# Sorting edges inside a language-model tower: larger pieces in the sort's trips through memory, ten dealing places, joint minimum and maximum operations

## The chip, the cores and the metric

The kernel runs on one core of a Trainium2 chip. A core has TensorE (PE, matrix products), VectorE (DVE, elementwise work and reductions), ScalarE (ACT, functions), GpSimd (POOL, here mostly indirect transfers) and SyncE (SP, which here only issues DMAs), and 16 DMA engines. The metric is the device time of one execution in microseconds (us). The kernel before has a median of 4921.01 us over 3 runs, from 4919.95 to 4923.06. The profile is of one further execution, which took 4925.54 us; its span from the first to the last instruction is 4923.8 us.

## The reference, cut to what matters

Two layers over 16,384 tokens of 64 features, all in float32. Each line adds to `h`:

```python
h = _L0_tok_ref(x, ...)                        # embedding and a small network
h = h + _L0_attn_ref(_layernorm(h), ...)       # a recurrence over 64 rows of 256 tokens
h = h + _L0_ffn_ref(_layernorm(h), ...)        # 8 experts, the best 2 per token
h = h + _L1_attn_ref(_layernorm(h), ...)       # attention in windows of 64
h = h + _L1_ffn_ref(_layernorm(h), ..., edge_index)
```

The last one is a graph layer, and it is what the sort is for. Each of 262,144 edges goes from a source token to a target token, and every target takes a softmax over its edges:

```python
e = leaky_relu(a_src[src] + a_dst[dst], negative_slope=0.2)
e_max = segment_max(e, dst, num_segments=M)
ee = exp(e - e_max[dst])
denom = segment_sum(ee, dst, num_segments=M)
agg = segment_sum(h[src] * (ee / (denom[dst] + 1e-16))[:, :, None], dst, num_segments=M)
```

The kernel sorts the edges by target, so that the segment sums become scans along sorted edges.

## The kernel before, in words

**Stages.** The tokens are worked on in two halves. For each half: 8 iterations of the recurrence (each two lanes of 512 tokens), a norm, 8 blocks of the experts, a norm, 16 iterations of attention, a norm, and a table of one row per token (`node_table`), which SP stores. When the first half's table is stored, GpSimd starts the edge work: 960 indirect gathers of table rows for the edges whose source lies in the first half, while the other engines do the second half; then it scatters target terms, gathers the rows of the other edges (1088), and gathers the segment ends (256). VectorE scans the rows as they come.

**The sort** runs beside the first half on VectorE. The keys (target, source and a flag in one word) lie as 128 partitions x 2048 in one of two buffers `K`, and it is a bitonic merge sort by a list of 192 steps from `network()`:

- `x`: an exchange at distance `d` along the 2048 keys of a partition, from one buffer to the other. For the first ten levels (55 steps, `up` not zero) the direction alternates along the row, and the step is four operations of 512 elements per partition (lines 1073, 1074); for the others it is one minimum and one maximum of 1024 elements (lines 1068, 1069).
- `sign`: one multiplication (line 1089) that turns the direction of a partition.
- `move`: keys of different partitions have to meet, so the buffer makes a trip through memory. VectorE only raises a signal (the copy at line 1092); SP waits for it, stores the buffer as it stands (`sort2`, line 314), waits until that has landed (line 315), and loads it back as 16-element pieces (`sortx`, line 316). There are 14 moves, two for each of 7 levels of merging across partitions. The next exchange waits for the load.

At the end come 3 more instructions (lines 1096 to 1098) that pick pivots; then `pivots()` counts them with TensorE, and its result (`key_block_idx`) starts GpSimd's 256 search gathers (line 457), which VectorE uses in attention (`search_round`).

**What sets the order.** Each engine has its own program, and the engines wait for one another by semaphores. VectorE's program is written out by hand: in `it(i)` each `step(...)` is one instruction for each of two lanes, preceded by its waits, and `burst(k)` puts sort steps in between. How many go where is worked out ahead by `sort_plan()` into `REC_AT` (recurrence: 7 places in each of 8 iterations), `PRE_AT` (before the experts), `FFN_AT` (4 quarters in each of 8 blocks of the experts) and `LEFT` (behind the experts). The plan assumes a time per step and per move, and deals no step before the move ahead of it should be over. SP works through its DMAs in program order, the gates of the experts among them, so that a move's wait stands in front of what follows in the queue.

The plan of before, as steps (moves) per iteration of the recurrence: 25, 25, 20 (2), 14 (1), 16 (2), 16 (2), 7 (1), 17 (2); 3 before the experts; 46 (4) in the experts; 4 behind them.

## Time and profile before

| | us |
|---|---|
| median of 3 runs | 4921.01 |
| the profiled execution, device time | 4925.54 |
| its span, first to last instruction | 4923.8 |
| 8 iterations of the recurrence, first half (36 to 790) | 754 |
| experts, first half (866 to 1093.5) | 227.5 |
| rest of the sort, pivots, norm (1093.5 to 1192) | 98.5 |
| attention, norm and table, first half (1192 to 1566) | 374 |
| from there to the end | 3357.8 |
| VectorE busy in the whole span | 2325.4 (47%) |
| GpSimd busy in the whole span | 2769.7 (56%) |

The stretches are cut by the starts of instructions in the trace, and the profiled execution's own time is the one that they belong to. A busy share over the whole span says little here: GpSimd does nothing in the first 1157 us and is the busiest engine behind them. The chain of work that ended last goes back from the last instruction, at each step to what released it. "issue" is time in which an engine waited for nothing that the profile shows.

### The profile page before, as it was taken

To read this page: it belongs to the slowest core of one execution; us is meant where nothing else is said; L and a number is where in the kernel's file an instruction comes from. 1 tells how busy PE (TensorE), PEld (TensorE's weight loads), DVE (VectorE), ACT (ScalarE), POOL (GpSimd) and SP (SyncE) were. 2 spreads that over 40 slices of the span, in tenths; PEclk is the share of its full clock that TensorE was granted. 3 is DMA by queue.
4 is the path that set the end of the run, shared out by engine and by line. 5 is a ranking of instruction groups with operands and counts; after the bars stand their busy time and mean duration, and the time that the engine had idled before them with its cause. 6 is when DMAs were issued, how large, how long until landed. Compare 5 with 4: busy or idle time off the path is not lost.

```text
span 4923.8 us, 70771 instructions
## 1 busy us (share of the span) xinstructions
PE 2410.7 (49%) x27920; PEld 1760.6 (36%) x27920; DVE 2325.4 (47%) x5102; ACT 1150.2 (23%) x2612; POOL 2769.7 (56%) x2870
## 2 busy tenths in 40 slices
PE   4666766764885788869688200024242424332000
PEld 3555655223663666753376100013131312121000
DVE  8867665778774344454677100023333242422336
ACT  2232332322442344435454000001010111100000
POOL 0000000004772777777777777777777777776775
PEclk8888887876886899979899555555555555555555
DMA  2033342750002911116211200112121212211122
GB/s 79 6 44 40 52 49 35 127 84 24 26 25 30 29 33 27 29 21 135 43 16 23 59 2 2 39 40 70 45 65 46 63 46 63 53 44 46 43 61 75
DMA packets 351882, 226.11 MB, mean 46 GB/s; under 512 B 215599, under 2 KB 311696, under 8 KB 349136
## 3 DMA queue, kind: packets, MB, share of 16 engines
q1 hardware_dynamic: 254272, 164.52, 16.9%
q0 software_dynamic: 92464, 49.28, 6.8%
q10 hardware_dynamic: 4896, 8.92, 0.7%
q8 instruction: 166, 2.72, 0.2%
q14 instruction: 84, 0.69, 0.1%
HBM read 136.08 MB, written 86.40 MB: 45 GB/s over the span
## 4 chain that ended last, share of the span: by engine, by line
POOL 50%; issue 19%; DVE 17%; PE 10%; DMA 3%; ACT 1%; POOLq 0%; SPq 0%; DVEq 0%
POOL arena L487 21%; POOL arena L470 19%; PE bank L501 10%; POOL arena L497 5%; POOL edge_dst_terms L479 5%; DVE arena L1069 3%; DVE arena L1068 2%; DMA arena<-sort_exchange 1%; DVE arena L1074 1%; DVE arena L1073 1%; DVE arena L1350 1%; DVE arena L1355 1%; DMA sort_exchange<-arena 0%; DVE arena L1203 0%; DVE arena L1079 0%
## 5 line engine op out<-in xcount | busy, mean ns | idle before, releaser
L501 PE MATMUL bank<-arena 64*64 64x64 f32 (+12 forms) x25222 | 2111.6, 291 | 1782.5 <-ACT arena L967 1184.0
L501 PEld LDWEIGHTS bank<-arena 64*64 64x64 f32 (+4 forms) x25222 | 1492.5, 164 | 2383.3 <-ACT arena L967 1257.3
L487 POOL DMA_INDIRECT arena<-node_table,arena x1088 | 1033.7, 950 | 331.6 <-issue 331.6
L470 POOL DMA_INDIRECT arena<-node_table,arena x960 | 942.1, 981 | 292.9 <-issue 292.3
L457 POOL DMA_INDIRECT arena<-sorted_keys,key_block_idx x256 | 257.1, 1004 | 444.4 <-DVE key_block_idx L1208 366.7
L450 POOL IOTA arena<- 128x1024 int32 x1 | 1.0, 989 | 781.6 <-DVE h_res L1153 781.6
L969 ACT ACTIVATE bank<-bank 128x512 f32<-128x512 f32 x32 | 18.6, 582 | 1413.5 <-DVE bank L1411 1413.5
L501 PE MATMUL bank<-ident,arena 128*128 128x128 f32 (+2 forms) x1792 | 235.2, 301 | 157.3 <-ACT arena L952 77.4
L1403 DVE COPY arena<-arena 128x4 f32<-128x4 f32 x32 | 5.8, 182 | 647.5 <-DMA arena<-node_table,arena 647.0
L497 POOL DMA_INDIRECT arena<-sums_sorted,arena x256 | 263.5, 1029 | 79.1 <-issue 77.7
L479 POOL DMA_INDIRECT edge_dst_terms<-arena x256 | 251.9, 984 | 84.5 <-issue 84.5
L501 PEld LDWEIGHTS bank<-ident,arena 128*128 128x128 f32 (+2 forms) x1792 | 209.8, 183 | 189.8 <-DVE arena L1356 104.2
L937 ACT ACTIVATE arena<-bank,arena 128x512 f32<-128x512 f32 x256 | 161.9, 684 | 220.4 <-PE bank L501 220.4
L1418 DVE TENSOR_TENSOR_SCAN arena<-bank,arena 128x64 f32<-128x64 f32 x640 | 179.0, 373 | 1.1
L1387 DVE TENSOR_TENSOR arena<-bank,arena 128x512 f32<-128x512 f32 x64 | 44.3, 692 | 267.2 <-PE bank L501 267.2
L1396 DVE COPY arena<-arena 128x4 f32<-128x4 f32 x1 | 0.2, 170 | 347.7 <-DMA arena<-edge_dst_terms 347.7
L1068 DVE TENSOR_TENSOR arena<-arena 128x1024 f32<-128x1024 f32 x116 | 141.7, 1221 | 37.6 <-DMA arena<-sort_exchange 34.9
L1312 DVE SCALAR_TENSOR_TENSOR arena<-bank,arena 128x512 f32<-128x512 f32 x128 | 90.2, 746 | 140.1 <-PE bank L501 81.2
L1069 DVE TENSOR_TENSOR arena<-arena 128x1024 f32<-128x1024 f32 x116 | 141.2, 1217 | 0.0
L967 ACT ACTIVATE arena<-bank,arena 128x512 f32<-128x512 f32 x128 | 84.5, 687 | 215.5 <-PE bank L501 215.3
L952 ACT ACTIVATE arena<-arena 128x512 f32<-128x512 f32 x128 | 77.5, 630 | 197.7 <-DVE arena L1356 197.7
L1350 DVE TENSOR_TENSOR arena<-bank,arena 128x512 f32<-128x512 f32 x128 | 80.0, 683 | 45.6 <-ACT arena L950 45.1
(377 smaller groups left out, 2789.2 us busy)
## 6 DMA issues: line engine op xcount, KB each, us to landing
arena<-expert_gates SPq DMA_DIRECT2D x64, 512.0 KB, 7.6
arena<-node_table,arena POOLq DMA_INDIRECT x2048
sums_sorted<-arena SPq DMA_DIRECT2D x32, 768.0 KB, 3.3
expert_out<-arena SPq DMA_DIRECT2D x64, 256.0 KB, 2.5
arena<-expert_out SPq DMA_DIRECT2D x16, 1024.0 KB, 5.6
sort_exchange<-arena SPq DMA_DIRECT2D x14, 1024.0 KB, 3.9
early_rows<-arena POOLq DMA_DIRECT2D x15, 768.0 KB
arena<-early_rows SPq DMA_DIRECT2D x15, 768.0 KB
```

The costliest lines, as they stand in the source:

```text
L457: G.indirect_dma_start(out=rows[:,u,:],out_offset=None,in_=keysb,in_offset=bass.IndirectOffsetOnAxis(ap=idx2[:,t:t+1],axis=0)).then_inc(s_ ...
L470: G.indirect_dma_start(out=early_b[j%2][:,c,:],out_offset=None,in_=tbl, in_offset=bass.IndirectOffsetOnAxis(ap=gidx[:,j*CW+c:j*CW+c+1],axi ...
L479: G.indirect_dma_start(out=ad_e,out_offset=bass.IndirectOffsetOnAxis(ap=sidx[:,h*NT+t:h*NT+t+1],axis=0), in_=nodeG[:,t,20:24],in_offset=No ...
L487: G.indirect_dma_start(out=rch[:,j%NB,c,:],out_offset=None,in_=tbl, in_offset=bass.IndirectOffsetOnAxis(ap=gidx[:,CA+j*CW+c:CA+j*CW+c+1],a ...
L497: G.indirect_dma_start(out=at[:,t,:],out_offset=None,in_=sums_d,in_offset=bass.IndirectOffsetOnAxis(ap=eidx[:,h*NT+t:h*NT+t+1],axis=0)).th ...
L501: mm=lambda o,a,b,st=True,sp_=True: nc.tensor.matmul(o,a,b,start=st,stop=sp_,skip_group_check=True)
L937: A.activation(B.hT[:,n%2,:],B.ps[n%2][:,:],ACT.Gelu,bias=fb1[:,n%8:n%8+1]).then_inc(B.ge,1)
L1068: V.tensor_tensor(y[:,:,0,:],x[:,:,0,:],x[:,:,1,:],ALU.min)
L1069: lk(V.tensor_tensor(y[:,:,1,:],x[:,:,0,:],x[:,:,1,:],ALU.max))
L1312: V.scalar_tensor_tensor(out=B.tm[:,q%2,:] if q else B.acc[:,k%2,:],in0=B.ps[2+m%2][:,:],scalar=fb2[l][:,q:q+1],in1=B.G[:,k%2,q,:],op0=ALU ...
L1350: step(lambda B,l:V.tensor_tensor(B.K,B.ps[0][:,P+D:2*P].unsqueeze(1).broadcast_to((P,8,D)),h8(hmask),ALU.mult),"act:q")
L1418: last=V.tensor_tensor_scan(R[:,:,f],xe[:,0,:,head(f)],R[:,:,f],cin[:,f:f+1],ALU.mult,ALU.add)
```

## The change

It touches only the sort, in four places. (1) In a move of level j the pieces have 2048/2^j keys instead of 16. On the way out (odd moves) they are stored as pieces and loaded as whole rows; on the way back (even moves) they are stored as whole rows and loaded as pieces. The distances of the exchanges between the two moves change with it. (2) Of the 55 exchanges in alternating directions 27 are written as one minimum and one maximum over 1024 elements. (3) `burst` has ten places instead of seven: one ahead of each of the three U additions is new, and the fifth stands four steps later. `sort_plan()` deals with other assumptions. (4) Behind the experts, the first steps up to the last move come ahead of the norm, the other 12 and the pivots behind it.

The new plan, as steps (moves) per iteration of the recurrence: 29, 29, 12 (2), 13 (1), 13 (1), 11 (2), 13 (1), 12 (1); 2 (1) before the experts; 43 (4) in the experts; 4 (1), then 12, behind them. By place, the first two iterations have 9, 2, 6, 3, 4, 1, 1, 1, 1, 1, and the fifth has 3, 0, 3, 1, 2, 1, 1, 1, 0, 1.

```diff
-        steps+=[("sign",j,0),("move",2*j-1,0)]+[("x",16<<b,0) for b in range(j-1,-1,-1)]
+        steps+=[("sign",j,0),("move",2*j-1,0)]+[("x",(RC>>j)<<b,0) for b in range(j-1,-1,-1)]
...
-PLACES=((2.0,9),(29.0,2),(40.0,5),(53.0,3),(64.0,4),(80.0,1),(92.0,1))
+PLACES=((1.7,8.0,(9,9,5,4)),(17.0,3.5,(2,2,1)),(24.0,6.0,(6,6,3)),(37.0,2.0,(3,3,1)),(46.0,4.0,(4,4,2)),
+        (52.5,2.0,(1,)),(55.0,2.0,(1,)),(57.5,2.0,(1,)),(62.0,0.3,(1,1,0)),(66.0,1.5,(1,)))
+REC_LEN=68.0; MOVE=[12.0]*8+[14.0]*2+[16.0]*2+[19.0]*2+[0.0]; FFN_LEN=22.0
...
-        sort2=sort_d.rearrange("(p c) -> p c",p=P); sortx=sort_d.rearrange("(p q l) -> q p l",p=P,q=P)
+        sort2=sort_d.rearrange("(p c) -> p c",p=P); sortx=[sort_d.rearrange("(q p l) -> p q l",p=P,q=1<<j) for j in range(XL+1)]
...
-                        sp.dma_start(sort2,K[k]).then_inc(s_st,16)
+                        j=(n+1)//2; parts=lambda t: t.rearrange("p (q l) -> p q l",q=1<<j)
+                        if n%2: sp.dma_start(sortx[j],parts(K[k])).then_inc(s_st,16)
+                        else: sp.dma_start(sort2,K[k]).then_inc(s_st,16)
                         sp.wait_ge(s_st,16*n)
-                        sp.dma_start(K[1-k].rearrange("p (q l) -> p q l",l=16),sortx).then_inc(s_sl,16)
+                        if n%2: sp.dma_start(K[1-k],sort2).then_inc(s_sl,16)
+                        else: sp.dma_start(parts(K[1-k]),sortx[j]).then_inc(s_sl,16)
...
+                    def part(t,at,step): return bass.AP(tensor=t.tensor,offset=t.offset+at,ap=[list(t.ap[0])]+[[st,n] for st,n in ((2*up,RC//(2*up)),(step,2),(2*d,up//(2*d)),(1,d)) if n>1])
+                    if 2*up==RC or up==2*d or d==1:
+                        lo,hi=part(x,0,up),part(x,d,up)
+                        V.tensor_tensor(part(y,0,up+d),lo,hi,ALU.min)
+                        lk(V.tensor_tensor(part(y,d,up-d),lo,hi,ALU.max))
...
                 for c in range(1,4):
+                    burst(4+c)
                     step(lambda B,l:V.tensor_tensor(B.U[:,c,:],B.ps[2][:,c*D:(c+1)*D],B.Wy[:,c,0,:],ALU.add),f"pe:U{c}","dve:W")
...
                 if part==0:
-                    steps_of((LEFT,0))
+                    steps_of((LEFT[0],0))
+                norm(part,H,xn)
+                if part==0:
+                    steps_of((LEFT[1],0))
                     pivots()
-                norm(part,H,xn)
```

What this moves on VectorE, in the order of its program. First the fifth iteration of the recurrence (counted from one) around the U additions, which are line 1142 of the kernel before and line 1169 of the changed one; lines 1139, 1140 and 1165, 1166 are the two additions ahead of them. Before:

```order
L1135 TENSOR_TENSOR arena<-arena 128x256 x2
L1136 TENSOR_TENSOR arena<-arena 128x256 x2
L1137 TENSOR_TENSOR arena<-arena 128x256 x2
L1138 TENSOR_TENSOR arena<-arena 128x256 x2
L1139 TENSOR_TENSOR arena<-bank,arena 128x512 x2
L1140 TENSOR_TENSOR arena<-bank,arena 128x512 x2
L1142 TENSOR_TENSOR arena<-bank,arena 128x64 x6
```

Now, with exchanges at lines 1088 and 1089:

```order
L1165 TENSOR_TENSOR arena<-bank,arena 128x512 x2
L1166 TENSOR_TENSOR arena<-bank,arena 128x512 x2
L1088 TENSOR_TENSOR arena<-arena 128x64x16
L1089 TENSOR_TENSOR arena<-arena 128x64x16
L1169 TENSOR_TENSOR arena<-bank,arena 128x64 x2
L1088 TENSOR_TENSOR arena<-arena 128x128x8
L1089 TENSOR_TENSOR arena<-arena 128x128x8
L1169 TENSOR_TENSOR arena<-bank,arena 128x64 x2
L1088 TENSOR_TENSOR arena<-arena 128x256x4
L1089 TENSOR_TENSOR arena<-arena 128x256x4
L1169 TENSOR_TENSOR arena<-bank,arena 128x64 x2
```

Three exchanges moved in between additions that stood in a row.

Then VectorE behind the experts: line 1299 (now 1326) adds the last expert results, lines 1096 to 1098 are the sort's last step, line 1203 and those ahead of it belong to the pivots; lines 1201 to 1206 are the norm of the changed kernel. Before:

```order
L1299 TENSOR_TENSOR h_res<-h_res,bank 128x4x64 x2
L1068 TENSOR_TENSOR arena<-arena 128x256x4
L1069 TENSOR_TENSOR arena<-arena 128x256x4
L1068 TENSOR_TENSOR arena<-arena 128x512x2
L1069 TENSOR_TENSOR arena<-arena 128x512x2
L1068 TENSOR_TENSOR arena<-arena 128x1024
L1069 TENSOR_TENSOR arena<-arena 128x1024
L1096 TENSOR_SCALAR pivot_ints<-arena 128x32
```

Now, from the last of the three exchanges that follow the experts:

```order
L1088 TENSOR_TENSOR arena<-arena 128x64x16
L1089 TENSOR_TENSOR arena<-arena 128x64x16
L1118 COPY rowbase<-rowp_f 128x1
L1201 TENSOR_REDUCE ln_stat<-h_res 128x32
L1202 SCALAR_TENSOR_TENSOR arena<-ln_stat,h_res 128x2048
L1204 TENSOR_REDUCE ln_stat<-arena 128x32
L1206 TENSOR_TENSOR arena<-arena,ln_stat 128x2048
L1201 TENSOR_REDUCE ln_stat<-h_res 128x32
L1202 SCALAR_TENSOR_TENSOR arena<-ln_stat,h_res 128x2048
L1204 TENSOR_REDUCE ln_stat<-arena 128x32
L1206 TENSOR_TENSOR arena<-arena,ln_stat 128x2048
L1088 TENSOR_TENSOR arena<-arena 128x1024
```

The norm, which stood behind the pivots, now stands between the last move (line 1118) and the eleven exchanges that follow it.

## Rows read from the trace of the kernel before

**Rows 1.** The chain that ended last, by line (page, part 4): shares of the span.

```profile
POOL arena L487 21%; POOL arena L470 19%; PE bank L501 10%; POOL arena L497 5%; POOL edge_dst_terms L479 5%; DVE arena L1069 3%; DVE arena L1068 2%; DMA arena<-sort_exchange 1%; DVE arena L1074 1%; DVE arena L1073 1%; DVE arena L1350 1%; DVE arena L1355 1%; DMA sort_exchange<-arena 0%; DVE arena L1203 0%; DVE arena L1079 0%
```

**Rows 2.** Busy time by stretch: stretch, length, PE, PEld, DVE, ACT, POOL, granted clock, DMA, GB/s.

```profile
36.00:790.00 754.00, 500.48 (x8896) 432.08 (x8896) 541.39 (x986) 231.38 (x561) 0.77 (x1) 0.83 0.24 34
...
866.00:1093.50 227.50, 161.53 (x600) 54.66 (x600) 175.04 (x214) 73.46 (x116) 0.00 (x0) 0.82 0.68 105
...
1566.00:4923.80 3357.80, 1390.75 (x14346) 993.57 (x14346) 1200.36 (x3011) 652.69 (x1413) 2506.20 (x2583) 0.63 0.23 45
...
2236.00:2385.00 149.00, 140.62 (x597) 44.70 (x598) 79.41 (x127) 73.45 (x116) 114.98 (x114) 0.96 0.61 124
```

**Rows 3.** GpSimd in order of time: start, duration (us), engine, line, operation [idle before, releaser].

```profile
1566.98 0.18 POOL L462 TENSOR_TENSOR pool_spare<-pool_spare 1x1 f32<-1x1 f32 x1 [75.22 <-DMA node_table<-arena]
```

**Rows 4.** Busy time by stretch, first and last of five iterations in the second half.

```profile
1747.60:1815.50 67.90, 55.77 (x1112) 47.66 (x1112) 29.81 (x77) 28.65 (x70) 51.86 (x54) 0.95 0.15 31
...
2024.40:2092.30 67.90, 55.60 (x1112) 47.48 (x1112) 29.92 (x78) 28.60 (x70) 51.66 (x55) 0.95 0.15 31
```

**Rows 5.** Busy time by stretch, two iterations of the recurrence in the first half.

```profile
143.40:249.30 105.90, 63.90 (x1112) 55.82 (x1112) 90.44 (x178) 28.90 (x70) 0.00 (x0) 0.81 0.03 6
...
611.20:693.00 81.80, 60.00 (x1112) 51.99 (x1112) 43.47 (x90) 28.76 (x70) 0.00 (x0) 0.87 0.45 47
```

**Rows 6.** VectorE in order of time, one iteration of the second half (no sort).

```profile
1757.35 0.43 DVE L1114 TENSOR_SCALAR arena<-arena 128x512 f32<-128x512 f32 x1 [8.10 <-ACT arena L867]
...
1762.64 0.86 DVE L1117 TENSOR_SCALAR arena<-bank 128x256 f32<-128x256 f32 x2 [1.35 <-PE bank L501]
1765.90 0.88 DVE L1118 SCALAR_TENSOR_TENSOR arena<-bank,arena 128x256 f32<-128x256 f32 x2 [2.40 <-ACT arena L877]
1777.39 0.69 DVE L1127 TENSOR_TENSOR arena<-bank,arena 128x512 f32<-128x512 f32 x1 [5.94 <-PE bank L501]
...
1787.00 0.42 DVE L1133 TENSOR_TENSOR arena<-bank,arena 128x256 f32<-128x256 f32 x1 [1.91 <-PE bank L501]
...
1796.97 0.69 DVE L1139 TENSOR_TENSOR arena<-bank,arena 128x512 f32<-128x512 f32 x1 [3.85 <-PE bank L501]
...
1802.29 0.39 DVE L1142 TENSOR_TENSOR arena<-bank,arena 128x64 f32<-128x64 f32 x2 [1.87 <-PE bank L501]
```

**Rows 7.** VectorE in order of time, first operations of two exchanges in four operations.

```profile
44.20 0.69 DVE L1073 TENSOR_TENSOR arena<-arena 128x512 f32<-128x512 f32 x1
...
46.73 0.69 DVE L1073 TENSOR_TENSOR arena<-arena 128x512 f32<-128x512 f32 x1
```

**Rows 8.** VectorE in order of time: sort's rest (two-operation exchanges), norm, line 1211.

```profile
1093.83 1.23 DVE L1068 TENSOR_TENSOR arena<-arena 128x1024 f32<-128x1024 f32 x1 [0.30 <-DVE h_res L1299]
...
1096.23 1.23 DVE L1068 TENSOR_TENSOR arena<-arena 128x1024 f32<-128x1024 f32 x1
...
1156.55 2.28 DVE L1174 TENSOR_REDUCE ln_stat<-h_res 128x32 f32<-128x2048 f32 x1
...
1180.42 1.23 DVE L1211 TENSOR_SCALAR arena<-arena 128x2048 int32<-128x2048 int32 x1
```

**Rows 9.** SP and TensorE in order of time around the move at 642 us.

```profile
647.89 0.67 SPq L316 DMA_DIRECT2D arena<-sort_exchange  x1
...
663.45 11.06 PE L501 MATMUL bank<-arena 64*64 64x64 f32 x198 [5.63 <-issue]
```

**Rows 10.** DMA issues: out<-in, queue, operation, count, KB each, median us to landing.

```profile
sort_exchange<-arena SPq DMA_DIRECT2D x14, 1024.0 KB, 3.9
...
arena<-sort_exchange SPq DMA_DIRECT2D x14, 0.1 KB, 14.2
...
end_positions<-arena SPq DMA_DIRECT2D x1, 128.0 KB
```

**Rows 11.** Waits between 862 and 1105 us: us in total, times, longest.

```profile
DVE arena L1068 <- DMA arena<-sort_exchange: 27.9, 4, 7.1
```

**Rows 12.** Waits of the SP queue, whole span.

```profile
SPq L369 <- DMA end_positions<-arena: 60.4, 1, 60.4
```

More of the change, by code:

```diff
@@ L65, in network, with take @@
     for j in range(1,XL+1):
-        steps+=[("sign",j,0),("move",2*j-1,0)]+[("x",16<<b,0) for b in range(j-1,-1,-1)]
+        steps+=[("sign",j,0),("move",2*j-1,0)]+[("x",(RC>>j)<<b,0) for b in range(j-1,-1,-1)]
         steps+=[("move",2*j,0)]+[("x",1<<b,0) for b in range(LOC-1,-1,-1)]
     return steps
-PLACES=((2.0,9),(29.0,2),(40.0,5),(53.0,3),(64.0,4),(80.0,1),(92.0,1))
-BEFORE_FFN=2
+PLACES=((1.7,8.0,(9,9,5,4)),(17.0,3.5,(2,2,1)),(24.0,6.0,(6,6,3)),(37.0,2.0,(3,3,1)),(46.0,4.0,(4,4,2)),
+        (52.5,2.0,(1,)),(55.0,2.0,(1,)),(57.5,2.0,(1,)),(62.0,0.3,(1,1,0)),(66.0,1.5,(1,)))
+REC_LEN=68.0; MOVE=[12.0]*8+[14.0]*2+[16.0]*2+[19.0]*2+[0.0]; FFN_LEN=22.0
 def sort_plan():
-    net=[kind for kind,d,up in network()]+["move"]
-    at=0; ready=0.0
-    def take(now,most):
-        nonlocal at,ready
-        n=m=0
-        while n<most and at<len(net) and now>=ready:
-            now+=2.4; n+=1
-            if net[at]=="move": ready=now+20.0; m+=1
+    net=network()+[("move",2*XL+1,0)]
+    at=0; now=38.0; ready=0.0
+    def take(most,hidden):
+        nonlocal at,now,ready
+        n=m=0; t=now
+        while n<most and at<len(net) and t>=ready:
+            kind,d,up=net[at]
+            t+=2.6 if up else dict(x=2.45,sign=1.4,move=0.2)[kind]; n+=1
+            if kind=="move": ready=t+MOVE[d-1]; m+=1
             at+=1
+        now=max(now,t-hidden)
         return n,m
-    rec=[[take(i*100.0+t,most) for t,most in PLACES] for i in range(ITA)]
-    t=ITA*100.0+10.0
-    pre=[take(t+30.0*k,3) for k in range(BEFORE_FFN)]
-    t+=30.0*BEFORE_FFN
-    ffn=[[take(t+36.0*k+9.0*q,2) for q in range(4)] for k in range(ITA)]
-    left=len(net)-at
-    return rec,pre,ffn,left
+    rec=[]
+    for i in range(ITA):
+        row=[]; prev=0.0
+        for off,hidden,most in PLACES:
+            now+=off-prev; prev=off
+            row.append(take(most[min(i,len(most)-1)],hidden))
+        now+=REC_LEN-prev
+        rec.append(row)
+    pre=[]
+    for t,most in ((22.0,0),(30.0,3)):
+        now+=t; pre.append(take(most,5.0))
+    now+=20.0
+    ffn=[]
+    for k in range(ITA):
+        row=[]
+        for q in range(4):
+            now+=FFN_LEN/4; row.append(take(2,2.0))
+        ffn.append(row)
+    rest=[kind for kind,d,up in net[at:]]
+    first=rest.index("move")+1
+    return rec,pre,ffn,(first,len(rest)-first)
 REC_AT,PRE_AT,FFN_AT,LEFT=sort_plan()
@@ L1070, in exchange @@
                 else:
-                    x,y=(t.rearrange("p (g u b w d) -> p g u b w d",u=2,b=up//(2*d),w=2,d=d) for t in (x,y))
-                    for u in range(2):
-                        V.tensor_tensor(y[:,:,u,:,0,:],x[:,:,u,:,0,:],x[:,:,u,:,1,:],ALU.max if u else ALU.min)
-                        last=V.tensor_tensor(y[:,:,u,:,1,:],x[:,:,u,:,0,:],x[:,:,u,:,1,:],ALU.min if u else ALU.max)
-                    lk(last)
+                    def part(t,at,step): return bass.AP(tensor=t.tensor,offset=t.offset+at,ap=[list(t.ap[0])]+[[st,n] for st,n in ((2*up,RC//(2*up)),(step,2),(2*d,up//(2*d)),(1,d)) if n>1])
[3 more added lines that the diff above has]
+                        lk(V.tensor_tensor(part(y,d,up-d),lo,hi,ALU.max))
+                    else:
+                        x,y=(t.rearrange("p (g u b w d) -> p g u b w d",u=2,b=up//(2*d),w=2,d=d) for t in (x,y))
+                        for u in range(2):
+                            V.tensor_tensor(y[:,:,u,:,0,:],x[:,:,u,:,0,:],x[:,:,u,:,1,:],ALU.max if u else ALU.min)
+                            last=V.tensor_tensor(y[:,:,u,:,1,:],x[:,:,u,:,0,:],x[:,:,u,:,1,:],ALU.min if u else ALU.max)
+                        lk(last)
             def below(t0,n,w,keys,c,out):
@@ L1133, in it @@
                 step(lambda B,l:V.tensor_tensor(B.dta[:,:,:],c4(B.ps[0][:,T:2*T]),B.dtb[:,:,:],ALU.add),"pe:x4","dve:d2")
-                step(lambda B,l:V.tensor_tensor(B.dtb[:,:,:],c4(B.ps[1][:,T:2*T]),B.dta[:,:,:],ALU.add),"pe:x8","dve:d4"); burst(4)
+                step(lambda B,l:V.tensor_tensor(B.dtb[:,:,:],c4(B.ps[1][:,T:2*T]),B.dta[:,:,:],ALU.add),"pe:x8","dve:d4")
                 step(lambda B,l:V.tensor_tensor(B.gtb[:,:,:],B.V[:,:,:],s4(B.bon[:,:]),ALU.mult),"act:bons")
@@ L1137, in it @@
                 step(lambda B,l:V.tensor_tensor(B.gtb[:,:,:],B.gtb[:,:,:],B.gt[:,:,:],ALU.mult),"act:gts","dve:gb")
-                step(lambda B,l:V.tensor_tensor(B.gt[:,:,:],B.gt[:,:,:],r4(rows[:,3,:],0),ALU.mult),"dve:gtb")
+                step(lambda B,l:V.tensor_tensor(B.gt[:,:,:],B.gt[:,:,:],r4(rows[:,3,:],0),ALU.mult),"dve:gtb"); burst(4)
                 step(lambda B,l:V.tensor_tensor(B.Z1[:,:,:,:],v3(B.ps[1][:,:]),B.Z0[:,:,:,:],ALU.add),"pe:Z1")
```

4 lines of the change are left out of this document (2 added, 2 removed).

## The prediction

> **What bounds the kernel now.** I read the chain of work that ended last first: its largest pieces are GpSimd's row gathers, lines 487, 470, 497 and 479 [rows 1]. The table of stages shows where they lie: from 1566 us to the end GpSimd is busy for 2506 of 3358 us, one indirect transfer after another [rows 2]. Nothing in that stretch is touched. It starts when GpSimd's wait of 75.22 us for the node table of the first half ends, at 1567 us [rows 3]. So the end follows the moment at which the table is stored, and before it lies a chain on TensorE, VectorE and ScalarE: 8 recurrence iterations (36 to 790 us), the first half's experts (866 to 1093.5 us), the sort's rest, the pivots and a norm (to 1192 us), attention (to 1566 us). VectorE deals the sort's 192 steps into this chain. What a step costs is what it takes beyond a gap in which VectorE would have waited anyway.
>
> The size of the gaps is in the second half, which runs the same loops without a sort: its undisturbed iterations take 68 to 70 us, 68.9 on average over five [rows 4], and its eight expert blocks 149 us [rows 2]. With the sort, the iteration from 143.4 us takes 105.9 us and the one from 611.2 us 81.8 us [rows 5], the expert blocks 227.5 us [rows 2]. That is the room: 753 against 551 us, 227.5 against 149 us.
>
> **A model of one iteration.** In an iteration without sort VectorE waits 8.10 us before line 1114 and 1.35 more before 1117 (some 10.5 us with three waits of under 0.6 us between), 2.40 before 1118, 5.94 before 1127, 1.91 before 1133, 3.85 before 1139, and 1.87 before each of the three U additions at 1142 [rows 6]; before 1150 and 1153 there is little (I take 0.5 and 1.6). An exchange in four operations repeats every 2.53 us [rows 7], one in two operations every 2.40 us [rows 8]. A place costs its steps less its gap, and not less than zero. For the iteration from 143.4 us (9, 2, 5, 3, 4, 1, 1 steps of 2.53) that is 12.3+2.7+6.7+5.7+6.3+2.1+0.9 = 36.7, with 68.9 it makes 105.6 us against 105.9 measured. So the model holds where no move runs. In iterations 2 to 7 it leaves 33 us unexplained, and these are the ones with moves: TensorE stands 5.63 us with nothing that the profile shows to wait for [rows 9], while the load of a move keeps the DMA engines full.
>
> **Part 1, ten places and another deal.** The recurrence gets 132 steps instead of 140. Iterations 0 and 1 get 29 each instead of 25, the others 11 to 13 instead of 7 to 20, and the three new places lie in the U gaps. Iterations 0 and 1: 9, 2, 6, 3, 4 and five single steps of 2.46 (half of them joint) cost 39 us, so 108 us each, 2 us more than now; with the 2 us by which the first is longer today that is 217.6. Iterations 2 to 7: 5 steps at the first place cost 1.5, 4 or 3 nothing; one at the second nothing; three at the third 1.2; one at the fourth 0.5; two at the fifth 0.9; a step before each U 0.5; one at the last 0.8. That gives 71.7, 71.5, 73.9, 72.5, 71.5, 73.9 = 435 us. Sum 652.6 against 753.1 now: 100.5 us less if no move disturbs. Moves still run: 8 instead of 10, of about 9 instead of 18 us (part 2), so of the 33 us I keep 33 x 0.8 x 0.47 = 12. **Term 1: -88 us, from -100 (no disturbance left) to -67 (all of it left).** The joint operations are in this: 27 of 55 exchanges become 0.13 us shorter, 3.5 us in all; a form of theirs that the trace does not show could cost nothing more, since the two and the four operation form differ only by their number.
>
> **Part 2, the moves.** Now every move stores 8 KB rows in 3.9 us and loads 64-byte pieces in 14.2 us [rows 10]: the same megabyte, 16,384 pieces, so small pieces are dear. After it, level j moves in pieces of 8192/2^j bytes, on the store side going out and on the load side coming back. As an estimate, linear in the pieces between those two rows, a side takes 4 us at levels 1 to 3, 5.2 at level 4, 6.5 at 5, 9 at 6, 14.2 at 7; with the other side and 0.5 us of signals a move takes 9 to 10 us at levels 1 to 4, 11, 13.5 and 18.6 at 5, 6 and 7. The deal leaves at least 13 us between a move and the next step in the recurrence, so VectorE should not wait there. In the expert blocks it now waits 27.9 us on four moves [rows 11]. Placed on the natural rhythm, the 43 steps there cost 50 us and the 46 of now 51 (the model gives 148.7+50.7+27.9 = 227.3 against 227.5 measured), and the gaps left for the four moves are 12.5, 14, 14 and 16 to 18 us. Only the store of level 7 should be late, by about 3 us. SP waits for each store before it loads, and the gates' loads queue behind; those are issued a block of 18 us ahead, so a store of up to 14 us is covered.
>
> The trace has no small stores of this size. The nearest row is a store of 32,768 single words, behind which SP waits 60.4 us [rows 10, 12], 1.84 us per thousand: 16,384 pieces would take at most 30 us by it, 14.2 us if a store costs what a load does. I take the second, the nearer in piece size; at the other end the last two stores make VectorE wait some 20 us longer. The Trainium skill has a rule against this change, in "DMA: Bandwidth & Descriptors", section Specifications: under 512 bytes a DMA engine reads, modifies and writes. No run here shows it yet; if it doubled the store of level 7, the forecast below would rise by about 14 us, inside the range. **Term 2: -25 us, from -28 to -5.**
>
> **Part 3, what is left.** 16 steps instead of 4 lie behind the expert blocks. Three and the last move come first, then the norm (24 us [rows 8], from 1156.55 us on, until 1180.4), under which the last move's 18.6 us are hidden; if it took 30 us, 6 would show. Then 11 exchanges of 2.40 us stand open: 26.4 us. The pivots themselves and SP's store ahead of them are unchanged. **Term 3: +26.5 us, from +25 to +32.** Since the norm now stands ahead of the pivots, GpSimd's search starts 24 us nearer to the table; its spare time there is 75 us [rows 3], so 51 are left and nothing is late. The step before the experts gets two steps instead of three, which a wait for TensorE hides in both cases: nothing.
>
> **Sum.** -88 - 25 + 26.5 = -86.5 us, on the profiled execution's 4925.5 us: 4839. The median of the runs, 4921.0, lies 4.5 us below that execution, so 4834.5. The bounds together give 4818 to 4879. The shift reaches the end whole, because both GpSimd's gathers and the second half of the dense work start from the table.
>
> **Rivals.**
> (a) The moves stay as long as now, because the piece is not what the DMA pays for. Against it: the two rows of one megabyte. Then VectorE waits 25 us in the recurrence (18 us per move against gaps of 13 to 15), the other 21 us of disturbance stay, and the expert blocks wait 14 us longer: +60, 4894.
> (b) Slower: a step costs the average wherever it stands, because VectorE's late answer also holds up TensorE and its clock (the granted clock is 0.81 in the iteration from 143.4 us, 0.87 in the one from 611.2 us [rows 5]). Today the recurrence pays (753-551)/140 = 1.44 us a step and the experts (227.5-149)/46 = 1.71. Then 132 and 43 steps give -12 and -5, and with +26.5 the kernel is 10 us slower: 4931. It turns slower from 1.37 us a step in the recurrence on. Against it: the model's 105.6.
> (c) The short gaps cost less than I count, no move disturbs anything and the clock stays at the second half's 0.95 [rows 4]: 4810.
>
> **Chances.** Forecast 0.77, (a) 0.09, (b) 0.06, (c) 0.08. The range reaches to (a) and to the better end of the forecast: 4815 to 4895. A measurement of this kernel tells about 0.2% (10 us) from no change: faster 0.92, within 0.2% 0.05 (half of (b) and a part of (a)), slower 0.03.
>
> **What would show it.** Right: iterations 2 to 7 of 71 to 76 us, no VectorE wait of over 3 us for the exchange in the recurrence, an expert stretch near 202 us, 11 exchanges behind the norm, GpSimd's wait for the table near 50 us. Wrong: moves over 13 us at levels 1 to 5, U steps that lengthen the iteration by their full 2.4 us, or a wait for the table of zero, by which GpSimd's search would have become the bound.

## The result, and the profile after

The changed kernel takes 4812.65 us (median of three runs, 4811.23 to 4815.97) against 4921.01 us: a ratio of 0.9779, with a 95% interval from 0.9766 to 0.9791. It is 108.4 us faster. The forecast was 86.5 us and its range began at 4815.0, so the time lies 2.4 us below the range: the sign, the three terms and their order were right, and the first term was too small.

The profiled execution took 4811.23 us with a span of 4809.5. Its stretches, as in [rows 2]: stretch, length, then busy time and instructions of PE, PEld, DVE, ACT and POOL, granted clock, mean share of the DMA engines, GB/s.

```profile
36.00:677.70 641.70, 475.24 (x8896) 407.32 (x8896) 520.34 (x916) 229.55 (x560) 0.00 (x0) 0.89 0.10 35
755.10:960.40 205.30, 161.42 (x600) 51.84 (x600) 168.32 (x208) 73.45 (x116) 0.00 (x0) 0.84 0.57 116
960.40:1085.30 124.90, 23.14 (x554) 19.84 (x555) 106.07 (x192) 8.32 (x17) 8.86 (x8) 0.50 0.20 36
1459.50:4809.50 3350.00, 1391.13 (x14346) 992.48 (x14346) 1201.42 (x3011) 652.59 (x1413) 2499.01 (x2583) 0.63 0.23 45
```

| stretch | before | after | difference | forecast |
|---|---|---|---|---|
| recurrence, first half | 753.2 | 641.8 | -111.4 | -88 |
| experts, first half | 227.3 | 205.3 | -22.0 | -25 |
| rest of the sort, pivots, norm | 98.4 | 124.9 | +26.5 | +26.5 |
| from the table to the end | 3356.8 | 3350.0 | -6.8 | 0 |

The two stretches that are left out, between the recurrence and the experts and from attention to the table, moved by +0.3 and -0.9 us. Most of the last line's 6.8 us is chance: that stretch is the same in every kernel here, and in the eleven other profiled executions it takes 3348 to 3356 us. The profiled execution of before lay 4.5 us above its median, that of after 1.4 below; the runs' medians are not touched by that.

The chain that ended last reads as in [rows 1]. GpSimd's wait for the table has shrunk from the 75.22 us of [rows 3] to 54.93 (forecast 51), so its search is still in time. In the order of the page's columns, the chain's shares by line, and GpSimd in order of time:

```profile
POOL arena L507 21%; POOL arena L490 20%; PE bank L521 10%; POOL arena L517 5%; POOL edge_dst_terms L499 5%; DVE arena L1089 2%; DVE arena L1088 1%; DVE arena L1100 1%; DMA sort_exchange<-arena 1%; DVE arena L1099 1%; DVE arena L1095 1%; DMA arena<-sort_exchange 1%; DVE arena L1379 1%; DVE arena L1384 1%; DVE arena L1094 1%
```

```profile
1459.52 0.18 POOL L482 TENSOR_TENSOR pool_spare<-pool_spare 1x1 f32<-1x1 f32 x1 [54.93 <-DMA node_table<-arena]
```

Iterations 2 to 7 now take 69 to 72 us, where that from 611.2 us took 81.8 [rows 5]; two of them:

```profile
322.80:392.00 69.20, 55.55 (x1112) 47.37 (x1112) 55.79 (x102) 28.57 (x70) 0.00 (x0) 0.98 0.12 40
392.00:463.30 71.30, 58.04 (x1112) 49.72 (x1112) 57.03 (x103) 28.66 (x70) 0.00 (x0) 0.93 0.11 39
```

The first has 13 sort steps in it and is about as long as an iteration of the second half that has none [rows 4]. Now the moves: the two of level 7, each with its store and its load (out<-in, queue, operation, count, KB each, median us from issue to landing; "1024.0 KB" or "0.1 KB" is the size of a piece as the view groups it).

```profile
sort_exchange<-arena SPq DMA_DIRECT2D x1, 1024.0 KB, 13.7
arena<-sort_exchange SPq DMA_DIRECT2D x1, 1024.0 KB, 4.7
...
sort_exchange<-arena SPq DMA_DIRECT2D x1, 1024.0 KB, 3.9
arena<-sort_exchange SPq DMA_DIRECT2D x1, 0.1 KB, 14.0
```

A megabyte in 64-byte pieces costs 13.7 us as a store and 14.0 as a load, so the price that the prediction took from [rows 10] for the unseen store was right. VectorE's waits for a move in the expert blocks fell from the 27.9 us of [rows 11] to this (us in total, times, longest):

```profile
DVE arena L1088 <- DMA arena<-sort_exchange: 8.5, 3, 4.0
```

In the recurrence VectorE waits for no move at all (before: 7.1 us in two waits), and TensorE's waits without a releaser, of which [rows 9] is one, went from 17.5 us in six to 1.1 us in one. The lines of before, then that of after:

```profile
DVE arena L1068 <- DMA arena<-sort_exchange: 7.1, 2, 6.2
PE bank L501 <- issue: 17.5, 6, 5.6
...
PE bank L521 <- issue: 1.1, 1, 1.1
```

### The profile page after: what moved, and what is told of

Its sections match the earlier page's. It is cut to its first block, busy times and chain, and to the rows that moved or that the text cites. A ratio compares the mean times of both kernels' runs of the same rounds, so it can differ in the third digit from the quotient of the medians.

```text
span 4809.5 us, 70708 instructions
## 1 busy us (share of the span) xinstructions
PE 2384.8 (50%) x27920; PEld 1731.6 (36%) x27920; DVE 2320.1 (48%) x5048; ACT 1149.3 (24%) x2612; POOL 2758.1 (57%) x2870
## 4 chain that ended last, share of the span: by engine, by line
POOL 51%; issue 19%; DVE 15%; PE 11%; DMA 2%; ACT 2%; POOLq 0%; SPq 0%; DVEq 0%
POOL arena L507 21%; POOL arena L490 20%; PE bank L521 10%; POOL arena L517 5%; POOL edge_dst_terms L499 5%; DVE arena L1089 2%; DVE arena L1088 1%; DVE arena L1100 1%; DMA sort_exchange<-arena 1%; DVE arena L1099 1%; DVE arena L1095 1%; DMA arena<-sort_exchange 1%; DVE arena L1379 1%; DVE arena L1384 1%; DVE arena L1094 1%
## 5 line engine op out<-in xcount | busy, mean ns | idle before, releaser
L521 PE MATMUL bank<-arena 64*64 64x64 f32 (+12 forms) x25222 | 2085.4, 288 | 1673.0 <-ACT arena L987 1182.6
L521 PEld LDWEIGHTS bank<-arena 64*64 64x64 f32 (+4 forms) x25222 | 1463.2, 161 | 2277.1 <-ACT arena L987 1255.8
L989 ACT ACTIVATE bank<-bank 128x512 f32<-128x512 f32 x32 | 18.6, 582 | 1408.1 <-DVE bank L1440 1408.1
L1088 DVE TENSOR_TENSOR arena<-arena 128x1024 f32<-128x1024 f32 x116 | 141.7, 1221 | 10.8 <-DMA arena<-sort_exchange 8.5
## 6 DMA issues: line engine op xcount, KB each, us to landing
arena<-expert_out SPq DMA_DIRECT2D x16, 1024.0 KB, 7.6
sort_exchange<-arena SPq DMA_DIRECT2D x14, 1024.0 KB, 5.1
```

Source lines behind the costliest of these rows:

```text
L521: mm=lambda o,a,b,st=True,sp_=True: nc.tensor.matmul(o,a,b,start=st,stop=sp_,skip_group_check=True)
L1088: V.tensor_tensor(y[:,:,0,:],x[:,:,0,:],x[:,:,1,:],ALU.min)
```

## Experiments

What had to be told apart: how much of the recurrence's 111 us comes from the pieces and how much from the places; what the "disturbance" of the prediction was, which it kept in part and which is gone; what a place is worth; and what the norm hides. Stretches below are cut as above, by the same instructions.

### Pieces against places

Two kernels fill in the square. The first is the changed kernel with the old pieces:

```diff
-        steps+=[("sign",j,0),("move",2*j-1,0)]+[("x",(RC>>j)<<b,0) for b in range(j-1,-1,-1)]
+        steps+=[("sign",j,0),("move",2*j-1,0)]+[("x",16<<b,0) for b in range(j-1,-1,-1)]
...
-                        if n%2: sp.dma_start(sortx[j],parts(K[k])).then_inc(s_st,16)
-                        else: sp.dma_start(sort2,K[k]).then_inc(s_st,16)
+                        sp.dma_start(sort2,K[k]).then_inc(s_st,16)
                         sp.wait_ge(s_st,16*n)
-                        if n%2: sp.dma_start(K[1-k],sort2).then_inc(s_sl,16)
-                        else: sp.dma_start(parts(K[1-k]),sortx[j]).then_inc(s_sl,16)
+                        sp.dma_start(K[1-k].rearrange("p (q l) -> p q l",l=16),sortx).then_inc(s_sl,16)
```

> The changed kernel with the moves of the kernel before (every store or load through DRAM that cuts the keys does it into 16-element pieces of 64 bytes); the new places, the new plan and the joint operations stay. Theory A (the small pieces slow the recurrence, beside the waits they cause): VectorE waits some 6 us for most of the eight moves that the recurrence hides, since the plan allows 12 us and a move took 3.9 and 14.2 us, and TensorE's queue shows the waits without a releaser again that the kernel before had (17.5 us in six waits); the recurrence goes from 641.8 to about 690 us (670 to 715), the experts' stretch from 205.3 to about 217 us, the whole to about 4872 us (4850 to 4890). Theory B (the recurrence was long before because of where the exchanges stood, and the pieces were nothing but a wait in the experts' stretch): recurrence within 10 us of 641.8, whole 4812 to 4835 us.

Measured: 4870.45 us, ratio 0.9895 (0.9878 to 0.9911). The stretches of the recurrence and the experts, then in the recurrence VectorE's waits for the moves and TensorE's waits without a releaser:

```profile
36.00:722.00 686.00, 485.70 (x8896) 417.85 (x8896) 519.86 (x916) 229.67 (x560) 0.00 (x0) 0.86 0.24 32
799.40:1015.30 215.90, 160.64 (x600) 51.93 (x600) 168.15 (x208) 73.35 (x116) 0.00 (x0) 0.83 0.69 111
```

```profile
DVE arena L1085 <- DMA arena<-sort_exchange: 28.7, 5, 6.8
...
PE bank L518 <- issue: 20.3, 3, 8.4
```

The second is the kernel before with the new pieces alone, the same lines the other way round.

> The kernel before with the new pieces alone; its places, its plan and its four-operation exchanges stay. Theory A (the small pieces were the disturbance of the recurrence): recurrence from 753.2 to about 718 us (712 to 728) with no wait without a releaser over 1 us on TensorE's queue, VectorE's 27.9 us of waits for the moves in the experts' stretch down to under 9 us and that stretch from 227.3 to about 205 us, the whole about 4865 us (4855 to 4880). Theory B (the disturbance came from the old places): recurrence within 10 us of 753.2, experts' stretch about 205 us, the whole about 4898 us (4890 to 4905).

Measured: 4885.93 us, ratio 0.9925 (0.9909 to 0.9942).

```profile
36.00:761.30 725.30, 499.84 (x8896) 431.39 (x8896) 540.23 (x983) 230.51 (x560) 0.00 (x0) 0.83 0.10 35
838.60:1056.00 217.40, 160.15 (x600) 52.12 (x600) 175.16 (x214) 73.45 (x116) 0.00 (x0) 0.85 0.59 110
```

```profile
DVE arena L1071 <- DMA arena<-sort_exchange: 18.5, 4, 7.5
```

| | recurrence, old pieces | new pieces | experts, old pieces | new pieces |
|---|---|---|---|---|
| old places and plan | 753.2 | 725.9 | 227.3 | 217.3 |
| new places and plan | 686.0 | 641.8 | 215.9 | 205.3 |

In the experts the two parts add: pieces 10.0 and 10.6 us, plan 11.4 and 12.0. The second kernel's whole came out 21 us above what was expected, 12 of them in the experts and 8 in the recurrence, where 726 lies near the upper end that was given. In the experts I had let the pieces take all but 9 of the 27.9 us of waits, but the old plan allows a move the same time at every level, so with it the long moves of the high levels still make VectorE wait 18.5 us. In the recurrence the parts do not add: the places are worth 67.2 us with the old pieces and 84.1 with the new, the pieces 27.3 us in the old places and 44.2 in the new, since the new plan leaves a move less room (with the old pieces VectorE waits 28.7 us for moves in the new plan, 7.1 in the old). For the recurrence Theory A holds in both kernels: with the new pieces TensorE has no wait without a releaser over 1.1 us in the new places, and none is listed in the old.

### What the disturbance was

An extra transfer that nobody waits for asks whether traffic alone does it. The changed kernel, with a copy behind each of the first eight moves:

```diff
+                        if n<=8:
...
+                            sp.wait_ge(s_sl,16*n)
+                            sp.dma_start(pad_d.rearrange("(p q l) -> p q l",p=P,l=16),tbl.rearrange("m f -> (m f)")[0:NE].rearrange("(q p l) -> p q l",p=P,l=16)).then_inc(s_pad,16)
```

> The changed kernel with eight extra copies, one behind each of the first eight moves: 512 KB of zeros from DRAM to DRAM in pieces of 64 bytes, which nothing in the computation reads and for which no engine but the queue waits. Theory A (64-byte traffic by itself slows the matmuls of the recurrence, whoever waits for it): waits without a releaser come back on TensorE's queue, 2 to 6 us for each copy, recurrence from 641.8 to about 670 us (655 to 690). Theory B (only waits for the moves and the places mattered): recurrence 641 to 648 us. Where a second move of an iteration lies behind a copy on the queue, VectorE may wait for that move as well; this shows as a wait for sort_exchange and is told apart.

(The expectation says 512 KB; a copy is 1 MB, like a move, in 16,384 pieces.) Measured: 4817.25 us, ratio 0.9785 (0.9769 to 0.9801), the changed kernel's own within the interval. The recurrence, and the stretch of the first copy alone:

```profile
36.00:678.70 642.70, 474.60 (x8896) 404.01 (x8896) 520.06 (x916) 229.43 (x560) 0.00 (x0) 0.89 0.35 48
300.80:316.00 15.20, 13.50 (x303) 12.32 (x299) 6.84 (x15) 4.36 (x12) 0.00 (x0) 1.00 1.45 110
```

```profile
PE bank L528 <- issue: 1.8, 3, 1.1
```

Theory A fell here: the share of the DMA engines is 1.45 (it adds up packets that overlap, so it passes 1), and TensorE is busy 13.5 of 15.2 us at the full clock. Full DMA engines are not the cause. What the old moves had and this does not is a load's direction, into the on-chip memory, and with it the form in which the pieces travel: the trace records a load in 64-byte pieces as 4096 packets of 256 bytes, a copy as 16,384 packets of 64. So the next kernel has loads in place of the copies, of the same size and the same pieces; direction and packets change together.

```diff
...
+                            sp.dma_start(pad.rearrange("p (q l) -> p q l",l=16),tbl.rearrange("m f -> (m f)")[0:P*2048].rearrange("(q p l) -> p q l",p=P,l=16)).then_inc(s_pad,16)
```

> The changed kernel with eight extra loads, one behind each of the first eight moves: 1 MB of zeros from DRAM into a part of the on-chip memory that nothing uses in the recurrence, in pieces of 64 bytes, as the old moves loaded them; no compute engine waits for them before the recurrence has ended. The old moves' loads came with waits of 4 to 8 us without a releaser on TensorE, while copies of the same pieces from DRAM to DRAM brought none over 1.1 us. Theory C (loads in 64-byte pieces into the on-chip memory hold up TensorE's instructions, whoever waits for the keys): two to four waits without a releaser of 4 to 9 us each on TensorE, recurrence from 641.8 to about 660 us (652 to 675). Theory D (TensorE stood still because the exchanges came late, and the profile only lacks the releaser): no such wait over 1.1 us, recurrence 641 to 648 us. In either case VectorE may wait for a second move of an iteration that is queued behind a load; this shows as a wait for sort_exchange and is told apart.

Measured: 4839.87 us, against 4809.6 for the changed kernel on the same chip: 30.3 us more. The recurrence is 32.7 us longer, and VectorE waits for no move in it. The recurrence, the 14.1 us of the first such load, and TensorE's waits:

```profile
36.00:710.40 674.40, 481.98 (x8896) 412.14 (x8896) 519.89 (x916) 229.49 (x560) 0.00 (x0) 0.87 0.29 45
300.20:314.30 14.10, 8.09 (x168) 7.25 (x163) 5.45 (x9) 2.37 (x7) 0.00 (x0) 0.85 1.21 103
```

```profile
PE bank L528 <- issue: 28.5, 7, 7.1
```

Theory C holds; the recurrence is at the upper end of what it allowed. The trace also shows what TensorE lacks. TensorE in order of time around the first of these waits:

```profile
308.52 0.56 PE L528 MATMUL bank<-arena 64*64 64x64 f32 x6 [0.59 <-DVE arena L1176]
316.16 2.13 PE L528 MATMUL bank<-arena 64*64 64x64 f32 x32 [7.09 <-issue]
```

The DMA queues between 312.5 and 313.0 us (queue, packets, MB, time as a share of 16 engines):

```profile
q1 hardware_dynamic: 150, 0.12, 231.2%
q8 instruction: 1, 0.02, 22.1%
```

One packet of the instruction queue starts at 312.5 us, and 3.7 us later TensorE goes on. So it is at each of the ten waits of over 4 us in three kernels: the packet starts 3.2 to 3.7 us ahead of the first matmul after the wait (before: 326.5, 660.0 and 736.5 us against 329.90, 663.45 and 740.11; with the old pieces 307.5, 541.5 and 617.5 against 311.21, 544.92 and 620.79; with the extra loads 312.5, 435.0, 538.5 and 618.5 against 316.16, 438.48, 541.72 and 621.92). The starts are read in steps of 0.5 us. The changed kernel moves 53 such packets in iterations 2 to 7, in which TensorE has 6 x 2224 = 13,344 instructions, 252 to a packet. The Trainium skill, "Advanced Engine Details and Errata", section ISA Cache, gives a cache line of 16 KB or 256 instructions, which fits both that count and the 0.02 MB of a packet.

That the packet comes late, three traces show side by side. The DMA queues from 300.5 to 312.5 us, in the changed kernel, with the copy running and with the load running:

```profile
q1 hardware_dynamic: 108, 0.75, 15.5%
q8 instruction: 3, 0.05, 1.4%
...
q1 hardware_dynamic: 14868, 0.95, 151.5%
q8 instruction: 2, 0.03, 1.6%
...
q1 hardware_dynamic: 3970, 1.02, 124.0%
```

In this stretch of the program three packets of the instruction queue start in the changed kernel and two beside the copy; beside the load there is none until 312.5 us. When a packet was asked for the trace does not show, so that it queued behind the load's pieces is inferred from these counts. Whether the direction does it or the form of the packets is not separated.

### What a place is worth

The changed kernel without the three places ahead of the U additions:

```diff
-        (52.5,2.0,(1,)),(55.0,2.0,(1,)),(57.5,2.0,(1,)),(62.0,0.3,(1,1,0)),(66.0,1.5,(1,)))
+        (52.5,2.0,(0,)),(55.0,2.0,(0,)),(57.5,2.0,(0,)),(62.0,0.3,(1,1,0)),(66.0,1.5,(1,)))
```

> The changed kernel without the three new places between the feed-forward results (offsets 52.5, 55 and 57.5): the plan then puts 111 steps in the recurrence instead of 132, and 38 are left behind the experts instead of 16, with one more move in the open. Theory A (a place is worth the gap it has): the 24 exchanges of these places cost about 0.45 us each in the recurrence, so the recurrence falls by about 11 us to 631 (625 to 637); the 22 more steps left open cost 2.40 us each, 53 us, and the fourteenth move is in the open, 18 us; the whole goes from 4812.65 to about 4872 us (4855 to 4885). Theory B (a step costs about the same wherever it stands): the recurrence falls by as much as the end grows, the whole 4805 to 4825 us.

Measured: 4891.73 us, ratio 0.9933 (0.9916 to 0.995). The recurrence and the stretch behind the experts, and VectorE's wait for moves in the latter:

```profile
36.00:673.50 637.50, 477.54 (x8896) 406.30 (x8896) 477.75 (x877) 229.39 (x560) 0.00 (x0) 0.88 0.09 28
951.00:1159.60 208.60, 23.07 (x553) 19.78 (x555) 152.56 (x233) 8.32 (x17) 8.90 (x9) 0.50 0.22 42
```

```profile
DVE arena L1088 <- DMA arena<-sort_exchange: 36.4, 2, 18.3
```

Theory B fell, and Theory A was too dear on the recurrence. The expectation counted 24 exchanges in these places; by the plan they hold 22 steps, of which 19 are exchanges, and the recurrence has 102 exchanges here instead of 120. The 18 fewer shorten it by 4.2 us, 0.2 us each, not by 11. The end grew by 83.7 us; I had counted one open move, and there are two. So an exchange in such a place saves 2.2 of its 2.4 us. VectorE's wait ahead of the U additions shows where it went: 44.8 us in 24 waits here, 7.3 in four with the places filled.

```profile
DVE arena L1169 <- PE bank L521: 44.8, 24, 2.3
...
DVE arena L1169 <- PE bank L521: 7.3, 4, 1.9
```

### The norm and the joint operations

The order of the end undone: all of the rest, the pivots, then the norm.

```diff
-                    steps_of((LEFT[0],0))
+                    steps_of((LEFT[0]+LEFT[1],0))
+                    pivots()
                 norm(part,H,xn)
-                if part==0:
-                    steps_of((LEFT[1],0))
-                    pivots()
```

> The changed kernel with the part behind the experts in the old order: all remaining exchanges, the pivots, and then the norm; sizes, places and plan stay. Theory A (the norm hid the fourteenth move): VectorE waits 17 to 19 us for that move in the open, so the stretch from the experts' end to the first product of the attention goes from 124.9 to about 143 us (140 to 145) and the whole from 4812.65 to about 4830 us (4826 to 4835). Theory B (that move is hidden by something else, or the pivots that come earlier let other work begin earlier): stretch and whole within 4 us of the changed kernel.

Measured: 4827.53 us, 17.9 above the changed kernel on the same chip; the stretch is 142.9 us, and the wait stands in the open:

```profile
DVE arena L1088 <- DMA arena<-sort_exchange: 18.0, 1, 18.0
DVE pivot_steps L1219 <- issue: 5.8, 1, 5.8
```

Theory A holds. Then the joint operations undone:

```diff
-                    if 2*up==RC or up==2*d or d==1:
+                    if up<0:
```

> The changed kernel with four operations again for each of the 55 exchanges that run both upward and downward blocks, where the changed kernel does 27 of them by two joint operations. An exchange of four half-size operations took 2.53 us in the trace of the kernel before, one of two operations 2.40 us. Theory A (the joint form is worth its own time where VectorE is full, in the first two iterations): these go from 216.7 us together (108.6 and 108.1) to about 220 us (218 to 222), nothing else moves, the whole is 4815.5 us (4812 to 4820). Theory B (fewer instructions matter by more than their time, since TensorE's operands wait behind them): the first two iterations together over 225 us.

Measured: 4819.04 us, ratio 0.98 (0.9786 to 0.9814). The first two iterations together take 222.3 us instead of 216.7:

```profile
36.00:258.30 222.30, 132.15 (x2224) 114.97 (x2224) 201.26 (x378) 57.81 (x140) 0.00 (x0) 0.79 0.02 6
```

That is 5.6 us, 0.3 above what was expected at most. Most of the excess is one exchange, the very first, VectorE in order of time:

```profile
37.48 1.08 DVE L1099 TENSOR_TENSOR arena<-arena 128x512 f32<-128x512 f32 x1
...
41.58 0.69 DVE L1099 TENSOR_TENSOR arena<-arena 128x512 f32<-128x512 f32 x1
```

It takes 4.10 us in four operations of 1.08, where all later ones take 2.53; as a joint pair it takes 2.39. Its operands are every fourth word of a row. 26 x 0.13 + 1.7 = 5.1 us. The kernel before had this exchange in the same form; the prediction had read the pace of two later ones [rows 7] and taken it for all.

### A version that is faster than both

The trace of after shows a gap that neither plan uses: VectorE waits 23.9 us for the gates ahead of the first expert. One more place there takes five exchanges and a move; the plan's allowances for the last six moves are brought near to what was measured:

```diff
-REC_LEN=68.0; MOVE=[12.0]*8+[14.0]*2+[16.0]*2+[19.0]*2+[0.0]; FFN_LEN=22.0
+REC_LEN=68.0; MOVE=[12.0]*8+[11.5,13.5,15.5,15.5,18.5,18.5]+[0.0]; FFN_LEN=22.0
...
     now+=20.0
+    g0=now; gap=take(9,24.0); now=g0+24.0
+    if gap[1]: ready=max(ready,g0+34.0)
...
+                    if part==0 and k==0: sort_moves(GAP_AT[1])
...
+                if part==0: steps_of(GAP_AT)
```

> The changed kernel with one more place: six steps (five exchanges and a move) in the 24 us in which VectorE waits for the gates before the first expert, the plan's allowances for the last six moves set to 11.5, 13.5, 15.5, 15.5, 18.5 and 18.5 us, and the plan made anew: 41 steps beside the experts instead of 43, and 11 exchanges behind them, all after the last move, instead of 14 and a move. The norm then stands behind the whole sort and hides the store of the pivots. Theory A (a place that has a gap gives back 2.40 us for each exchange of the open end): the stretch behind the experts goes from 124.9 to about 112 us (three exchanges, 7.2 us, and the 5.7 us for which the pivots' store was waited), the experts' stretch stays within 4 us of 205.3, the gates' loads come at the same time, the whole is 4800 us (4795 to 4805). Theory B (exchanges in that gap delay the gates, or the move collides with the gates' loads): the first expert starts over 3 us later after the gates, and the whole stays within 5 us of the changed kernel.

> The changed kernel itself, unaltered, so that the others of this group are compared with it on one chip: 4812.65 us, within 0.2% (4803 to 4822).

Measured: 4802.76 us (4800.17 to 4803.17), and 4809.60 (4806.76 to 4810.56) for the changed kernel. The whole came as expected, the stretch did not: 121.4 us instead of 112, since the last move was late and its end stood ahead of the norm, in the open. What was missing there the experts gave: 200.7 us instead of 205.3, with two steps fewer beside them, a little more than the 4 us that the expectation allowed. The first expert started when it did before, and VectorE's wait ahead of it halved, from 23.9 to 11.6 us:

```profile
DVE arena L1343 <- DMA arena<-expert_gates: 15.7, 2, 11.6
...
DVE arena L1091 <- DMA arena<-sort_exchange: 9.9, 1, 9.9
```

So the rest of the sort went between the norm's two halves:

```diff
-                if part==0:
-                    steps_of((LEFT[0],0))
-                norm(part,H,xn)
...
+                norm(part,H,xn,between=(lambda: steps_of((LEFT[0]+LEFT[1],0))) if part==0 else None)
+                if part==0: pivots()
...
```

> The kernel with the place in the gates' gap, and the remaining 11 exchanges and the store of the pivots now stand between the two halves of the norm. With the norm behind them, VectorE had waited 9.9 us in the open for the last move. Theory A (the first half of the norm, some 12 us, hides the end of the last move, and the second half hides the pivots' store): no wait over 1 us for sort_exchange behind the experts and none of 5.7 us before the pivots' differences, the stretch from the experts' end to the first product of the attention goes from 121.4 to about 111.5 us (110 to 113), the whole from 4802.8 to about 4793 us (4789 to 4797). Theory B (TensorE's products of the norm's first half or ScalarE's part of it are needed sooner, so the split norm costs as much as it hides): the whole within 3 us of 4802.8.

> The kernel with the place in the gates' gap, unaltered, so that the split norm is compared with it on one chip: 4802.8 us, within 0.2% (4793 to 4812).

Measured: 4797.19 us (4795.72 to 4799.01), ratio to the kernel before 0.9755 (0.9741 to 0.9769); 4805.25 (4803.37 to 4813.74) without the split. Theory A holds: both waits are gone, and the stretch is 111.8 us.

```profile
956.80:1068.60 111.80, 23.16 (x555) 19.86 (x557) 98.80 (x186) 8.31 (x17) 8.87 (x8) 0.50 0.15 27
```

Beside the changed kernel this is 12 us less, some 120 in all. The whole lies 0.2 us above what was expected at most.

## Why the prediction was right or wrong

**Term 1, the recurrence: the mechanism right, the size wrong.** It was to give 88 us and gave 111.4, beyond the 100 that were named as its best. 652.6 + 12 us were forecast and 641.8 measured, and the missing 22.8 us have three parts. Twelve are the disturbance that the term kept in proportion to the moves that remain. With pieces of 512 bytes and more there is next to none (1.1 us in one wait): it came from loads in 64-byte pieces, which the recurrence no longer makes, and not from moves as such. The case "no disturbance left" was named as the bound, and was the fact; the proportion, 33 x 0.8 x 0.47, had no row behind it. Ten more are the charges of the places in iterations 2 to 7: 435 us forecast, 425.0 measured, and three of the six iterations lie under the 71 us that were named as the least. The prediction charged 0.5 us for each exchange ahead of a U addition there, some 6.5 us for 13 of them; in the kernel without these places the six iterations have 12 exchanges fewer and take 423.4 us, 1.7 less. So about five of the ten lie in the U places; in which of the other places the rest lies no run takes apart. Why an exchange of 2.4 us behind a wait of 1.87 costs less than their difference was not isolated either: TensorE's waits for the U additions grow from 4.5 to 13.3 us with these places, yet the recurrence as a whole grows by 4.2. The last 0.9 us lie in iterations 0 and 1, 216.7 against 217.6; by the four-operation kernel the joint form is worth 5.6 us there, not 3.5.

One part of the 111 us the prediction has no term for: TensorE's 8896 matmuls of the recurrence take 475.2 us at a granted clock of 0.89, where they took 500.5 at 0.83 [rows 2]. No run holds the clock fixed, so whether it is a cause of the shorter iterations or only follows from them stays open.

**The disturbance itself was put at 33 us and was 27.3**, by the kernel with the new pieces in the old places. The model of one iteration had been fitted where no move runs, so all that it missed in the others went into that one number.

**Term 2, the experts: right,** -22.0 against -25. The price of a store in small pieces was the term's open point, with 30 us at one end; 13.7 against a load's 14.0 settles it. The Trainium skill's rule in "DMA: Bandwidth & Descriptors", section Specifications, that an engine reads, modifies and writes under 512 bytes, had been weighed against the change. This case's traces show no surcharge for it on a store, 13.7 us against the load's 14.0 in 64-byte pieces; whether it has a part in the price of both they do not show. The store of level 7, which was to make VectorE wait 3 us, did not; three moves of levels 5 and 6 did, by 8.5 us. Half of the term is due to the pieces and half to the plan that knows the levels, which the prediction had not told apart.

**Term 3, the end: right,** +26.5, and for the reason given: without the norm over it, the last move costs 17.9 us more, where 18.6 had been put down. That it is right to the tenth is luck.

**The rivals.** (a), moves as long as now, fell with the prices above; it was worked out to +60 us, and the kernel with the old pieces, which is such a case, measures 57.8 over the changed one, with the 25 us of waits (28.7), the 21 of disturbance (20.3 of TensorE's waits) and the 14 in the experts (10.6) that were put down for it. (b), a step costs the same anywhere, is refuted by the kernel without the U places: 0.2 against 2.4 us. (c), short gaps cheaper and no disturbance, 4810 us, had a chance of 0.08 and is what happened, but for its clock: 0.89 over the recurrence, 0.92 to 0.98 in iterations 2 to 7, where (c) had 0.95.

**The range.** Its low end, 4815, stood above (c), although (c) needed only two small errors with one sign. The sum of the best ends of the three terms was 4818 by the same working, so the range left the better side hardly any room, and all its width went to the other. (The worst ends add up to 4881, not 4879.)

## What to carry to other kernels

Cut the pieces of a transfer as large as the step allows, also where nobody waits for it: loads in pieces of 64 bytes into the on-chip memory held up TensorE's instructions, which the profile shows only as waits without a releaser and as a packet of the instruction queue in each of them. A filler step is worth its place: 0.2 us in a gap that the engine has anyway, 2.4 in the open. When an effect is to be scaled, ask first which property carries it, since a disturbance that belongs to the piece's size vanishes with it and is not left in proportion to the number of transfers.

## What the runs showed of the hardware

- A load of 1 MB in 64-byte pieces into the on-chip memory can stop TensorE for 4.3 to 8.4 us: ten of the 26 such loads in the recurrences of three kernels did. Beside copies of the same pieces from DRAM to DRAM, with a DMA share of 1.45 against the load's 1.21, no such wait is over 1.1 us, and one of 1.1 us stands in the changed kernel too.
- 1 MB in one direction, by piece: 3.9 us at 8 KB (store), 5.5 (store) and 6.3 (load) at 512 bytes, 6.2 and 8.8 at 256, 10.2 and 10.8 at 128, 13.7 and 14.0 at 64. Each is one transfer, and the load at 256 and both at 128 ran among the experts' gate loads. Between 8 KB and 64 bytes the price rises less than fourfold.
- A minimum of 512 elements whose operands are every fourth word of a row took 1.08 us, where the denser patterns of the other exchanges took 0.69. The Trainium skill, "SBUF — State Buffer", section "Door 1: The DMA port swizzle", speaks of lines of 16 bytes that run at full speed with at least two accesses to each; four words are such a line, and the trace agrees.
